# A Mamba scan on one core: a third buffer for sums and exponentials, first taps on GpSimd, and work of unit starts and of batch 1 moved ahead

## What is computed

```python
x = x + 0.5 * ffn(layernorm(x)); x = x + attention(layernorm(x)); x = x + 0.5 * ffn(layernorm(x))
x = x + 0.5 * moe(layernorm(x)); x = x + mamba(layernorm(x)); x = x + 0.5 * moe(layernorm(x))
```

```python
z, xBC, dt = split(u @ Wi.T)                       # 256, 512 and 4 columns
xBC = silu(conv1d(xBC, conv_w, 4 taps) + conv_b)   # depthwise, causal
x, B, C = split(xBC); dt = softplus(dt + dt_bias)  # x: 4 heads x 64
h = h * exp(dt * A) + (dt * x) * B                 # step by step
y = h . C + D * x
y = rmsnorm(y * silu(z)) * norm_w; out = y @ Wo.T
```

## Time and profile before

| | us |
|---|---|
| median of 3 runs (lowest, highest) | 825.32 (821.44, 828.21) |
| the profiled execution | 819.01 |
| its span | 817.2 |
| busy in it: PE, ACT, DVE, POOL | 715.5, 542.0, 489.4, 275.2 |

### The profile page before, as it was taken

One profiled execution on the slowest core, in us unless ns is written; L12 is line 12 of the kernel. 1 busy time (PEld: TensorE's weight loads), 2 busy tenths in 40 slices (PEclk: granted clock), 3 DMA queues, 4 the chain that ended last, 5 costly groups with the idle time before them and its releaser, 6 DMA issues. The chain is left out here.

```text
span 817.2 us, 13088 instructions
## 1 busy us (share of the span) xinstructions
PE 715.5 (88%) x4076; PEld 377.9 (46%) x4076; DVE 489.4 (60%) x1424; ACT 542.0 (66%) x934; POOL 275.2 (34%) x296
## 2 busy tenths in 40 slices
PE   4799999979999997988988867798888987999996
PEld 1432222212223223555655545576575775566564
DVE  6878442204766565763466649789697875533453
ACT  5367998888998993653357666885987642434441
POOL 3090003301000342435522445343443380265552
PEclk9899999999999997999999988899998898999999
DMA  4056934521493311112121031121211231222233
GB/s 136 1 203 165 186 86 88 207 76 53 138 317 85 110 37 40 44 34 62 42 80 46 26 109 60 52 65 53 74 60 50 81 84 39 65 61 57 67 99 92
DMA packets 76409, 70.10 MB, mean 86 GB/s; under 512 B 9687, under 2 KB 60233, under 8 KB 76080
## 3 DMA queue, kind: packets, MB, share of 16 engines
q1 hardware_dynamic: 71024, 60.56, 26.6%
q0 software_dynamic: 5024, 8.54, 3.2%
q10 hardware_dynamic: 288, 0.10, 0.0%
HBM read 41.23 MB, written 29.02 MB: 86 GB/s over the span
## 5 line engine op out<-in xcount | busy, mean ns | idle before, releaser
L693 ACT ACTIVATE attn_p<-attn_ps 128x1024 f32<-128x1024 f32 x256 | 241.1, 1083 | 28.5 <-PE attn_ps L686 17.2
L709 PE MATMUL attn_ps<-attn_p,attn_v 128*32 128x512 f32 x1024 | 138.1, 611 | 5.5 <-issue 5.5
L1687 PE MATMUL ps_main<-moe_xsT,moe_w 128*128 128x320 f32 x384 | 127.9, 459 | 8.5 <-DVE moe_hid L1712 3.3
L1697 ACT ACTIVATE moe_act_h<-ps_main 128x320 f32<-128x320 f32 (+1 forms) x128 | 55.2, 434 | 102.5 <-PE ps_main L1687 72.2
L1712 DVE TENSOR_TENSOR moe_hid<-moe_act_h,ps_main 128x320 f32<-128x320 f32 (+1 forms) x128 | 61.9, 485 | 91.1 <-ACT moe_act_h L1697 57.4
L1580 POOL DMA_INDIRECT moe_slots<-rows,moe_scatter_at x64 | 63.4, 991 | 103.0 <-DVE moe_hid L1712 53.8
L1687 PEld LDWEIGHTS ps_main<-moe_xsT,moe_w 128*128 128x128 f32 x384 | 68.8, 195 | 42.5 <-issue 21.8
L686 PE MATMUL attn_ps<-attn_q_rows,attn_k_rows 64*128 64x512 bf16 x448 | 80.6, 388 | 6.4 <-issue 3.1
L1717 PE MATMUL ps_main<-moe_hid,moe_w 128*128 128x320 f32 (+1 forms) x256 | 73.3, 451 | 4.6 <-DVE moe_hid L1712 4.6
L686 PEld LDWEIGHTS attn_ps<-attn_q_rows,attn_k_rows 64*128 64x128 bf16 x448 | 19.1, 93 | 124.0 <-ACT attn_p L693 99.0
L2119 DVE SCALAR_TENSOR_TENSOR mb_act<-mb_padded,mb_taps,mb_act 128x1024 f32<-128x1024 f32 x48 | 65.9, 1382 | 9.0 <-ACT mb_act L2110 8.3
(11 more groups left out here) (268 smaller groups left out, 1304.5 us busy)
## 6 DMA issues: line engine op xcount, KB each, us to landing
...
```

The lines of the kernel that those rows point to most:

```text
L693: self.core.nc.scalar.activation(self.p[:, w % self.PB, :, :].rearrange("p a n -> p (a n)"), self.ps_s[:, w % self.SB, :, :].rearrange("p ...
L709: ins = self.core.nc.tensor.matmul(self.ps_av[32 * i:32 * i + 32, :], self.v[:, b * TPB + kt, (HGROUPS * i + m) // 2, self.window(m)], sel ...
L1687: self.core.nc.tensor.matmul(ps[:, w % 2, 0:CAP], wt[:, e, c * P:(c + 1) * P], self.xsT[:, u % 2, :], start=True, stop=True).then_inc(self ...
L1697: self.core.nc.scalar.activation(self.act_h[into, w % 2, :], self.ps_h1[rows, w % 2, 0:CAP], ACT.Silu).then_inc(self.silu_done, 1)
```

## The change

- `cums` and `e_seg` get a third place, lent from `moe.hid` (free after the last expert of the first MoE layer); `spread_sums`, the relus (now `lower`) and the exponential (now `exps`) run two chunks ahead. The copy of B (`copy_b`) stays one chunk ahead, between the two.
- For units 1 to 3 the first taps of pieces 0 to 3 are made on GpSimd (`first_tap_beside`): piece 0's ahead of the gate at step 0, the others behind the decay at steps 1, 2, 3.
- Piece 0 of unit u+2 is projected and copied out at step 7 of unit u (that of unit 1 ahead of the scan), not at step 0 of unit u+1.
- Batch 1: `combine` and statistics from steps 3, 4 to 1, 2 of unit 0; root and normalisation from step 6 to 4; TensorE's turns and ScalarE's copies from step 7 to 5; `steps`, the first part of `step_sizes` and `exp_dt` to step 7 of unit 0; the rest of `step_sizes` to step 0 of unit 1; `sums` and `exp_sums` to step 1.

The diff, cut to its core:

```diff
--- before.py
+++ after.py
@@ -1895,7 +1895,7 @@
         self.lowered = sem("lowered")
-        self.cums_in, self.e_cum_in = ([sem(f"{n}{i}") for i in range(2)] for n in ("cums_in", "e_cum_in"))
+        self.cums_in, self.e_cum_in = [sem(f"cums_in{i}") for i in range(3)], [sem(f"e_cum_in{i}") for i in range(2)]
         (self.gm_done, self.mt_done, self.xw_done, self.h_decayed, self.h_ready, self.y_read, self.gate_done) = (
@@ -1992,9 +1992,11 @@
         j = n % TPB
-        if g >= 2:
-            sp.wait_ge(self.lowered, g - 1)
-        sp.dma_start(self.cums[:, g % 2, :, :], self.cum_dram[b, di, j].unsqueeze(0).to_broadcast([P, NH, P])).then_inc(self.cums_in[g % 2], 16)
+        if g == 2:
+            sp.wait_ge(self.core.moe.y_done, B * E_)
+        if g >= 3:
+            sp.wait_ge(self.lowered, g - 2)
+        sp.dma_start(self.cums[g % 3], self.cum_dram[b, di, j].unsqueeze(0).to_broadcast([P, NH, P])).then_inc(self.cums_in[g % 3], 16)
@@ -2109,6 +2111,13 @@
+    def first_tap_beside(self, pool, u, c):
+        src, tap = self.window(u, c, 0)
+        pool.wait_ge(self.proj_read, (u * self.PIECES + c) * 2 + 2)
+        if u >= 2:
+            pool.wait_ge(self.y_read, self.NC * (u - 1))
+        self.core.nc.gpsimd.tensor_scalar(self.act_t[:, u % 2, c, :], src, tap, 1.0, ALU.mult, ALU.mult).then_inc(self.tapped, 1)
+
     def convolve(self, dve, ch, u, c, k):
@@ -2147,23 +2156,27 @@
-    def exps(self, act, g):
+    def lower(self, act, g):
...
         u, di, b, i, n, cols = self.at(g)
-        act.wait_ge(self.cums_in[g % 2], 16 * (g // 2 + 1))
+        act.wait_ge(self.cums_in[g % 3], 16 * (g // 3 + 1))
         act.wait_ge(self.decays, self.DECAYS * (b + 1))
-        if g >= 2:
-            act.wait_ge(self.mt_done, g - 1)
+        if g >= 3:
+            act.wait_ge(self.mt_done, g - 2)
         for hh in range(NH):
-            ins = nc.scalar.activation(self.e_seg[:, g % 2, hh, :], self.cums[:, g % 2, hh, :], ACT.Relu, bias=self.cum[:, di, n, hh:hh + 1], scale=-1.0)
+            ins = nc.scalar.activation(self.e_seg[g % 3][:, hh, :], self.cums[g % 3][:, hh, :], ACT.Relu, bias=self.cum[:, di, n, hh:hh + 1], scale=-1.0)
         ins.then_inc(self.lowered, 1)
+
+    def copy_b(self, act, g):
         act.wait_ge(self.b_done, g + 1)
...
             act.wait_ge(self.st_done, self.passed(g - 2))
-        nc.scalar.copy(self.bs[:, g % 2, :], self.ps_b[:, 0:P]).then_inc(self.b_read, 1)
+        self.core.nc.scalar.copy(self.bs[:, g % 2, :], self.ps_b[:, 0:P]).then_inc(self.b_read, 1)
+
+    def exps(self, act, g):
         act.wait_ge(self.lowered, g + 1)
-        nc.scalar.activation(self.e_seg[:, g % 2, :, :], self.e_seg[:, g % 2, :, :], ACT.Exp, scale=-1.0).then_inc(self.seg_exp, 1)
+        self.core.nc.scalar.activation(self.e_seg[g % 3], self.e_seg[g % 3], ACT.Exp, scale=-1.0).then_inc(self.seg_exp, 1)
@@ -2188,7 +2201,7 @@
         dve.wait_ge(self.gm_done, g + 1)
-        nc.vector.tensor_tensor(self.mt[:, g % 2, :, :], self.e_seg[:, g % 2, :, :], self.gm[:, g % 2, :].unsqueeze(1).to_broadcast([P, NH, P]),
+        nc.vector.tensor_tensor(self.mt[:, g % 2, :, :], self.e_seg[g % 3], self.gm[:, g % 2, :].unsqueeze(1).to_broadcast([P, NH, P]),
                                 ALU.mult).then_inc(self.mt_done, 1)
@@ -2374,6 +2387,7 @@
         moe.yT = [lent[:, 1, :, :].rearrange("p h t -> p (h t)")[:, 0:CAP] for lent in (mamba.e_seg, mamba.mt)]
+        mamba.e_seg, mamba.cums = ([own[:, 0, :, :], own[:, 1, :, :], moe.hid[:, 1, :, i * P:(i + 1) * P]] for i, own in enumerate((mamba.e_seg, mamba.cums)))
         mamba.skips, mamba.cum_rows = moe.hid[:, 0, 0:2, 0:2 * P], moe.back[0:2 * TPB * NH, 0, 0:2, :]
@@ -2449,6 +2463,7 @@
                 mamba.before(pe, 0)
+                mamba.project(pe, 1, 0)
                 for g in range(N):
@@ -2464,15 +2479,19 @@
                         pe.wait_ge(norm.ready, 20)
+                    if u == 0 and i == 5:
+                        norm.turn(pe, 18)
+                        norm.turn(pe, 19)
                     if u + 1 < UNITS:
                         for c in mamba.PIECES_AT[i]:
-                            mamba.project(pe, u + 1, c)
+                            if c:
+                                mamba.project(pe, u + 1, c)
+                    if u + 2 < UNITS and i == 7:
+                        mamba.project(pe, u + 2, 0)
                     if u == 0 and i == 7:
-                        norm.turn(pe, 18)
-                        norm.turn(pe, 19)
+                        pe.wait_ge(norm.ready, 20)
+                        mamba.steps(pe, 1)
                     if u == 1 and i == 1:
-                        mamba.steps(pe, 1)
-                    if u == 1 and i == 3:
                         mamba.sums(pe, 1)
@@ -2542,14 +2561,15 @@
                             mamba.spread_decays(sp, g)
+                        mamba.spread_sums(sp, 2)
                         moe.fetch(sp, 1)
-                        for g in range(2, N + 1):
+                        for g in range(3, N + 2):
                             if g == 2 * NC:
...
                                 mamba.spread_sums(sp, g)
-                            if g >= 3:
-                                mamba.spread_decays(sp, g - 1)
+                            if g >= 4:
+                                mamba.spread_decays(sp, g - 2)
                 for half in range(2):
@@ -2578,10 +2598,14 @@
                         mamba.to_state(pool, g + 1)
+                    if u < 3 and i == 0:
+                        mamba.first_tap_beside(pool, u + 1, 0)
                     if u < 3:
...
                         mamba.decay(pool, g + 1)
+                    if u < 3 and i in (1, 2, 3):
+                        mamba.first_tap_beside(pool, u + 1, i)
                     if u == 3 and 2 <= i <= 6:
@@ -2674,15 +2698,15 @@
                             mamba.convolve(dve, ch, u + 1, c, k)
-                    if u == 0 and i in (3, 4):
-                        moe.combine(dve, ch, 1, i - 3)
-                        norm.stats_of(dve, ch, i + 15)
-                    if u == 0 and i == 6:
+                    if u == 0 and i in (1, 2):
+                        moe.combine(dve, ch, 1, i - 1)
+                        norm.stats_of(dve, ch, i + 17)
+                    if u == 0 and i == 4:
                         norm.normalise(dve, ch, 18)
                         norm.normalise(dve, ch, 19)
-                    if u == 1 and i == 1:
+                    if u == 0 and i == 7:
                         mamba.step_sizes(dve, ch, 1, 0)
-                    if u == 1 and i == 2:
+                    if u == 1 and i == 0:
                         for part in range(1, mamba.STEP_PARTS):
@@ -2780,14 +2804,23 @@
                 mamba.take(act, 0, 5)
+                mamba.lower(act, 0)
+                mamba.copy_b(act, 0)
                 mamba.exps(act, 0)
+                mamba.take(act, 1, 0)
+                mamba.lower(act, 1)
+                mamba.exps(act, 1)
                 for g in range(N):
                     u, i = g // NC, g % NC
+                    if g + 2 < N:
+                        mamba.lower(act, g + 2)
                     if g + 1 < N:
-                        mamba.exps(act, g + 1)
+                        mamba.copy_b(act, g + 1)
+                    if g + 2 < N:
+                        mamba.exps(act, g + 2)
                     if g == 1:
                         act.wait_ge(moe.y_out[(HALF - 2) % moe.OUT], moe.landings(HALF - 2))
-                    if u == 0 and i == mamba.GATES_AT:
+                    if u == 0 and i == 4:
                         norm.root(act, 18)
@@ -2802,20 +2835,21 @@
                         for c in mamba.PIECES_AT[i]:
-                            if c < 4:
+                            if 1 <= c < 4:
                                 mamba.take(act, u + 1, c)
-                                mamba.first_tap(act, u + 1, c)
                         if gates:
...
                             mamba.square(act, g - 1)
-                    if u == 0 and i == 7:
+                    if u == 0 and i == 5:
                         norm.copy(act, nc.scalar.copy, 18)
                         norm.copy(act, nc.scalar.copy, 19)
-                    if u == 1 and i == 2:
+                    if u + 2 < UNITS and i == 7:
+                        mamba.take(act, u + 2, 0)
+                    if u == 0 and i == 7:
                         mamba.exp_dt(act, 1)
-                    if u == 1 and i == 4:
+                    if u == 1 and i == 1:
                         mamba.exp_sums(act, 1)
```

## The result

| us | before | changed |
|---|---|---|
| median of 20 runs each (lowest, highest) | 821.3 (816.01, 828.21) | 827.41 (821.56, 833.98) |
| span of the profiled execution | 817.2 | 824.9 |

The ratio is 1.0069, with a 95% interval of 1.0046 to 1.0093: slower by some 5.7 us (3.8 to 7.7), inside the 1% named as "same". The forecast was +6.2 us. The 831.5 us that it named was counted from a median before of 825.3; the 20 runs have 821.3.

What follows compares the result with a forecast made beforehand. VectorE was taken to bound steps with taps, with 24 us of waits at unit ends as target. Terms +5.7 +3.6 -3.0 +2.9 +0.2 -1.9 -0.7 -0.6 = +6.2 us: 825 against the profile's 819, or 831.5 from median 825.3; range 822 to 843.

Steps and rivals of the forecast that it cites:

- Start: Start of the scan: unit 1's early piece 0 removes a 3.93 us stall, partly given back; together -3.0 us.
- steps 2 and 3: GpSimd's taps of pieces 2 and 3 block VectorE's two-input operations: 0.6 us, six times, +3.6 us.
- norm: Normalisation of tiles 18 and 19, moved from step 6 to step 4 on VectorE, the bound engine: net +2.9 us.
- step 1: Units 0 to 2: VectorE waits for GpSimd's tap behind gate and decay, 1.9 us three times, +5.7 us.
- Rival (b): A GpSimd tap costs 2.37 us, like its two-input form: +21 us, 846 us; chance 0.16.
- Rival (c): One-input GpSimd taps don't block VectorE, only step 1's order costs: +2.6 us, 828 us; chance 0.20.
- now starts near 488.5: +0.6: Within the start: piece 1's GpSimd tap, otherwise at 487.95, waits for ScalarE's copy behind the sums: +0.6 us.
- End of unit 0: Exponential wait goes, but TensorE's projection and `steps` come ahead of before(9); xdt(9) near 534.0, +0.2 us.
- End of unit 1: No `steps` there; xdt(17) near 583.25, first taps near 585.9 for 588.12, 0.35 back: -1.9 us.
- +1.8 (projection): End of unit 1: TensorE's projection, between the squares and before, priced at 1.8 us.
- End of unit 2: Exponential waits go, but logits wait for ScalarE's norm copy and the gate for its square: -0.7 us.
- Step sizes: Batch 1: part 0 of the step sizes falls into a wait of VectorE, -0.6 us.

Runs made afterwards that it cites:

- the filler alone: Kernel before with only piece 5's two matmuls (units 1 to 3) done twice, where TensorE idles beside ScalarE's silus; ratio 0.9997, before -0.2 us.
- The run with the filler: Changed kernel with piece 5's two matmuls (units 1 to 3) done twice, where TensorE idles beside ScalarE's silus; ratio 1.0031, before +2.6 us.

## Why the prediction was right, and where its terms were off

**Right in sum and sign, with luck in the sum.** +6.2 us was forecast and +5.7 measured. Start, steps 2 and 3 and norm came 4.1 us below their terms, the three ends of units 5.9 above. That these cancel to within 2 us is luck; the term that carries the sign, step 1, was right.

**Step 1, +5.7.** Shown. 1.9 us each time in the trace, by the order gate, decay, tap. The sum of lengths behind it (4.82 us for the pair) was measured as 4.84 to 4.86. With the tap ahead of the gate 2.03 us go in unit 2 and 0.6 in unit 1, none in unit 0 where the copy is late; with the taps on ScalarE 5.8 go in all, and both kernels are level with before. Rival (b) is out by the tap's 1.11 us against my 1.04.

**Steps 2 and 3, +3.6.** Mis-sized: +1.9 in the trace. Rival (c) is out as a rule, since in unit 0 L1825 (the second half of a combine) took 1.49 us beside a tap for 0.69 without, and mt 1.47 for 0.96; but in unit 1 the same two steps lost nothing. There the taps took 2.19 and 2.09 us for 1.11 beside VectorE's pairs, which kept their 2.60 and 2.83: it was GpSimd that waited.

```profile
498.71 1.49 DVE L1825 TENSOR_TENSOR x_sb<-x_sb,moe_back 128x512 f32<-128x512 f32 x1
...
558.27 2.19 POOL L2119 TENSOR_SCALAR mb_act<-mb_padded,mb_taps 128x1024 f32<-128x1024 f32 x1 [1.59 <-ACT mb_padded L2099]
```

I had let VectorE pay each time; about half the price came. In unit 2 the run with the taps ahead of the gate puts 0.44 us on everything but the order.

**The start, -3.0.** The size was right: the traces have -4.5, but before's profile had 1.6 us more there than the runs with the third place or the filler alone (xdt(2) at 14.92 after xdt(0), for 13.31 and 13.29), and against those the changed kernel's 10.33 is -3.0. The step "now starts near 488.5: +0.6" did not come. The sums were to land at 485.14 as before, and ScalarE took them up at 483.00; GpSimd's tap of piece 1 started at 487.03, right behind the decay. That landing varies: over the kernels of this case it lies 11.4 to 13.7 us after xdt(0). In the run with the projection beside the silus, at 12.6, xdt(2) to xdt(3) took 10.53 us for 10.12; how a later one would hit the changed kernel, no run shows. Where the tap stands ahead of the gate or on ScalarE, the late copy does hurt, and there the early start was worth 0.15 us at xdt(7).

**Norm, +2.9.** 2.55 us on VectorE, 0.57 of it given back at the silus: +2.0.

**End of unit 0, +0.2.** The reading was right: xdt(9) at 534.78 for the 534.0 forecast, behind L1940. It became +1.1: the clock was 0.79 from xdt(8) to xdt(9), and the first pair of taps beside gate and decay took 3.29 us for 2.60, 0.69 more where I had 0.35. With `steps` away 1.90 us come back, for 1.8 assumed, at a clock of 1.00.

**End of unit 1, -1.9.** This is the step that failed: "+1.8 (projection)". It took 3.62 us, the squares and outputs ahead of it were longer too, and xdt(17) came at 588.90 in place of 583.25 (2.6 of it from the delays before). The term became +1.6. I priced the projection from a row at the full clock, although it was to stand shortly behind TensorE's idle beside the silus. The run with the filler tests this: at full clock the stretch takes 4.40 us, where the forecast had 4.55 (578.70 to 583.25). End of unit 2 became +0.8 for -0.7. xdt(23) to xdt(25) took 11.54 us at clocks of 0.68 and 0.74, and 9.36 with the filler at 0.97 and 1.00, so it has most likely the same cause.

**Step sizes, -0.6.** As forecast.

**What stays open.** Each kernel was profiled once, and the stretches of low clock fall elsewhere in each; the split of the +5.7 us over terms of under 2 us is that of two executions. Why the taps ahead of the gate gained 5.2 us in the times and 1.8 in the trace, and why the norm's return measured as a gain while its trace shows none, was not settled. A filler of another size was not tried.
